# Attention and mixture of experts on one core: from all experts over all rows to experts over rows sorted by routing

## The reference

```python
def reference(x, ...):                       # x: (32, 256, 128) float32
    # attention: 16 heads of size 8
    qkv = (x @ W_qkv.T + b_qkv).reshape(B, T, 16, 24)
    att = softmax(einsum('bthd,bshd->bhts', q, k) / sqrt(8))
    x = layernorm(x + einsum('bhts,bshd->bthd', att, v) @ W_out.T + b_out)
    # mixture of 8 experts, 2 for each row, and one shared expert
    scores = sigmoid(x @ gate_w.T)
    sel = top_k(scores + expert_bias, 2)
    top_scores = scores at sel
    for each row and each of its 2 experts e:
        routed = row * score
        h = silu(routed @ w1[e].T) * (routed @ w3[e].T)
        out_r = (h @ w2[e].T) * score
    shared = silu(x @ sw1.T) * (x @ sw3.T) @ sw2.T
    return layernorm(x + shared + sum of the row's two out_r)
```

## Time and profile before

| | |
|---|---|
| profiled execution | 847.3 us, of it 845.5 us span |
| median of the runs | 844.6 us |
| PE | 762.4 us (90%), 6228 matmuls |
| VectorE | 708.3 us (84%) |
| ScalarE | 579.6 us (69%) |
| POOL | 472.3 us (56%) |
| DMA | 109.36 MB, mean 129 GB/s |
| last gate logits | 469 us |

### The profile page before, as it was taken

The page is one execution under the profiler, slowest core; times in us unless marked ns, Lnnn a source line. Parts: engine busy times, 40 slices in busy tenths (PEclk is TensorE's granted clock), DMA queues, the critical chain, the costliest instruction groups (busy, mean ns, idle before and its releaser), DMA issues.

```text
span 845.5 us, 19602 instructions
## 1 busy us (share of the span) xinstructions
PE 762.4 (90%) x6228; PEld 472.6 (56%) x6228; DVE 708.3 (84%) x1430; ACT 579.6 (69%) x1192; POOL 472.3 (56%) x687
## 2 busy tenths in 40 slices
PE   2598999999999999999987889989999999999894
PEld 1234555555555555555545566666666666666662
DVE  5577999999999999999983688888888787887885
ACT  1038999998989999899884566555555655565551
POOL 3336654554555456455212466666766766666664
PEclk9998999999999999999998899999999999999997
DMA  5754767676777677676412633334444544444430
GB/s 156 161 121 105 168 170 168 148 167 169 164 155 178 149 165 167 171 161 144 103 34 68 172 91 91 107 99 104 119 119 110 124 124 124 124 124 121 116 86 26
DMA packets 201682, 109.36 MB, mean 129 GB/s; under 512 B 10496, under 2 KB 201088, under 8 KB 201600
## 3 DMA queue, kind: packets, MB, share of 16 engines
q1 hardware_dynamic: 200048, 105.88, 51.7%
q10 hardware_dynamic: 1552, 2.44, 1.0%
HBM read 73.94 MB, written 33.82 MB: 127 GB/s over the span
## 4 chain that ended last, share of the span: by engine, by line
PE 60%; DVE 11%; POOL 9%; issue 8%; DMA 7%; ACT 2%; SPq 1%; DVEq 1%; POOLq 0%; ACTq 0%
PE bank L732 15%; PE bank L704 10%; PE bank L717 7%; DMA probs<-route_dram 5%; PE bank L739 4%; PE bank L741 3%; PE bank L740 3%; DVE k_stack L1083 3%; POOL place L510 3%; POOL rstd L519 3%; PE bank L814 2%; PE bank L897 2%; PE bank L794 2%; PE bank L834 2%; PE bank L801 2%
## 5 line engine op out<-in xcount | busy, mean ns | idle before, releaser
L1009 DVE TENSOR_REDUCE negmax<-bank 128x2 f32<-128x512 f32 x512 | 320.3, 679 | 31.2 <-PE bank L717 28.7
L558 ACT ACTIVATE probs<-bank 128x512 f32<-128x512 f32 x512 | 291.4, 606 | 44.8 <-PE bank L704 41.1
L717 PE MATMUL bank<-k_stack,q_stack 48*128 48x256 bf16 x1024 | 164.2, 284 | 11.4 <-DMA k_stack<-k_parts_dram 7.3
L704 PE MATMUL bank<-q_stack,k_stack 50*128 50x256 bf16 x1024 | 158.0, 276 | 7.6 <-ACT probs L558 6.1
L739 PE MATMUL bank<-x_hi,hi_w 128*128 128x512 f32 x288 | 137.6, 478 | 14.8 <-DVE k_stack L1083 9.5
L732 PE MATMUL bank<-probs,v_aug 128*32 128x256 f32 x2048 | 139.4, 390 | 0.4 <-ACT attT L569 0.4
L1073 DVE TENSOR_TENSOR k_stack<-bank,probs 128x512 f32<-128x512 f32 x128 | 87.6, 684 | 49.1 <-DMA probs<-route_dram 31.5
L704 PEld LDWEIGHTS bank<-q_stack,k_stack 50*128 50x128 bf16 x1024 | 75.6, 95 | 92.5 <-ACT probs L558 48.5
L741 PE MATMUL bank<-x_lo,hi_w 128*128 128x512 f32 x288 | 114.4, 397 | 0.0
L740 PE MATMUL bank<-x_hi,lo_w 128*128 128x512 f32 x288 | 114.0, 396 | 0.0
L510 POOL TENSOR_TENSOR k_stack<-k_stack,probs 128x512 f32<-128x512 f32 x48 | 62.0, 1293 | 79.1 <-DVE k_stack L1083 71.3
(11 more groups left out here) (116 smaller groups left out, 1338.7 us busy)
## 6 DMA issues: line engine op xcount, KB each, us to landing
probs<-route_dram SPq DMA_DIRECT2D x128, 256.0 KB, 6.0
q_stack<-q_parts_dram SPq DMA_DIRECT2D x64, 192.0 KB, 3.7
k_stack<-k_parts_dram SPq DMA_DIRECT2D x64, 192.0 KB, 4.9
k_parts_dram<-k_parts SPq DMA_DIRECT2D x32, 192.0 KB, 2.2
q_parts_dram<-q_parts SPq DMA_DIRECT2D x32, 192.0 KB, 2.2
xT_sb<-xT SPq DMA_DIRECT2D x32, 128.0 KB, 2.2
k_parts_dram<-k_parts SPq DMA_DIRECT2D x32, 128.0 KB, 2.0
q_parts_dram<-q_parts SPq DMA_DIRECT2D x32, 128.0 KB, 2.2
```

Source lines behind the costliest of these rows:

```text
L558: nc.scalar.activation(probs[h][:], score_ps[EXP_BANK[h]][:].rearrange("p (j t) -> p j t", j=NT), ACT.Exp).then_inc(exp_done, 1)
L704: mm = pe.matmul(score_ps[EXP_BANK[h]][:, j * T:(j + 1) * T], k_stack[b.ring][first:last, h // 2, j * P:(j + 1) * P], q_stack[b.ring][firs ...
L717: mm = pe.matmul(max_ps[MAX_BANK[h]][:, i * T:(i + 1) * T], q_stack[b.ring][first:last, h // 2, i * P:(i + 1) * P], k_stack[b.ring][first: ...
L1009: nc.vector.tensor_reduce(negmax[b.ring % 2][:, :, column], max_ps[MAX_BANK[h]][:].rearrange("p (i s) -> p i s", i=NT), AX_X, ALU.max, neg ...
```

## The change

Each expert now sees only its rows. The 32 batches are cut into five chunks of 6, 8, 8, 6 and 4 batches (12, 16, 16, 12 and 8 tiles). When the logits of a chunk are there, VectorE routes it in 26 small steps spread over the heads of one slot, four slots after the chunk's last batch (slots 9, 17, 25 and 31; the last chunk's after the slots): both choices as before, then running counts of each expert's rows, and for each row the two places in a DRAM table (rows_dram) in which every expert's rows stand in blocks of 128. Two small bf16 matmuls add the counts over partitions. Empty places must be blank: ScalarE's queue writes zeros to the tables, two quads a slot from slot -2. POOL sends each tile's rows (132 numbers wide: 128, and the score) with indirect DMAs, one per tile and choice, 128 in all: four a slot (two before x_bo, two at the end), eight from slot 28 on. The copy into x1T, x1_dram and the products of slot 33 go.

```diff
+        def scatter_plan():
+
+            queue, plan = [], {}
+            for s in range(-4, B + 3):
+                for c in chunks[:-1]:
+                    if s == c.last + ROUTE_SLOT + 1:
+                        queue += [(c, choice, i) for choice in range(2) for i in range(c.n)]
+                for place in range(2):
+                    many = 2 if s < B - 4 else 4
+                    plan[s, place], queue = queue[:many], queue[many:]
+            return plan, queue + [(chunks[-1], choice, i) for choice in range(2) for i in range(chunks[-1].n)]
+
+        SCATTERS, LAST_SCATTERS = scatter_plan()
```

```diff
+            def scatter(c, choice, i):
+                if i == 0 and choice == 0:
+                    pool.wait_ge(route_step, steps(c, 23))
+                    pool.wait_ge(blanked[c.c], 16 * c.quads)
+                if i == 0 and choice == 1:
+                    pool.wait_ge(rows_out[c.c][0], 16 * c.n)
+                if i == 0:
+                    pool.tensor_copy(x1_rows[:, c.t0:c.t0 + c.n, C], scores_of(c, choice)).then_inc(score_put, 1)
+                    pool.wait_ge(score_put, 2 * c.c + choice + 1)
+                pool.indirect_dma_start(c.rows_dram, bass.IndirectOffsetOnAxis(ap=slot_column(c, choice, i), axis=0),
+                                        x1_rows[:, c.t0 + i, :], None).then_inc(rows_out[c.c][choice], 16)
+
+            def scatters(s, place):
+                if s == 1 and place == 0:
+                    tables()
+                for c, choice, i in SCATTERS[s, place]:
+                    scatter(c, choice, i)
...
+                scatters(t.s, 0)
...
-                if b.live:
-                    pool.wait_ge(x1T_set, b.count(1, 1))
-                    pool.tensor_copy(x1T[:, bass.ds(b.n * T, T)], x1T_new[:]).then_inc(x1T_kept, 1)
+                            pool.tensor_tensor(w_lo[m][:], w_stage[m][:], w_hi[m][:], ALU.subtract).then_inc(w_lo_set, 1)
+                scatters(t.s, 1)
 
             slots(pool, slot)
...
+            for c, choice, i in LAST_SCATTERS:
+                scatter(c, choice, i)
+
+            def gather(g):
+
+                c = chunk_of_group(g)
+                if g == c.groups[0]:
+                    for r in range(2):
+                        pool.wait_ge(y_kept[r], kept(c, r))
+                if g >= GY:
+                    pool.wait_ge(combined, 2 * GT * (g - GY + 1))
+                for choice in range(2):
+                    for i in range(GT):
+                        column = slot_column(c, choice, g * GT + i - c.t0)
+                        pool.indirect_dma_start(gathered[g % GY][:, choice * GT + i, :], None, c.y_dram,
+                                                bass.IndirectOffsetOnAxis(ap=column, axis=0)).then_inc(gather_in[g % GY], 16)
+
+            def root(c):
+                pool.wait_ge(eps2_set, c.c + 1)
+                tiles = slice(c.t0, c.t0 + c.n)
```

```diff
+            def load_rows(k):
+                c = chunk_of_quad(k)
+                for choice in range(2):
+                    sp.wait_ge(rows_out[c.c][choice], 16 * c.n)
+                if k == 0:
+                    for other in chunks:
+                        sp.wait_ge(blanked[other.c], 16 * other.quads)
+                if k >= XQ:
+                    sp.wait_ge(xT_T, k - XQ + 1)
+                    sp.wait_ge(hid_set, 4 * (k - XQ + 1))
+                q = k - c.k0
+                sp.dma_start(xq[k % XQ][:], c.rows_dram[4 * P * q:4 * P * (q + 1), :].rearrange("(a p) c -> p a c", p=P)
+                             ).then_inc(xq_in[k % XQ], 16)
+
+            def keep_products(k):
+                c = chunk_of_quad(k)
+                q = k - c.k0
+                sp.wait_ge(yq_set, k + 1)
+                sp.dma_start(c.y_dram[4 * P * q:4 * P * (q + 1), :].rearrange("(a p) c -> p a c", p=P),
+                             y_q[k % 2].rearrange("p (a c) -> p a c", c=C)).then_inc(y_kept[k % 2], 16)
```

```diff
+            def blanks(first):
+                for k in range(max(first, 0), min(first + BLANKS, QUADS)):
+                    c = chunk_of_quad(k)
+                    if k == 0:
+                        act_e.wait_ge(blank_set, 1)
+                    act_e.dma_start(c.rows_dram[4 * P * (k - c.k0):4 * P * (k - c.k0 + 1), :].rearrange("(p a) c -> p a c", a=4),
+                                    xq[0][:]).then_inc(blanked[c.c], 16)
...
+            def rows_to_sbuf(k):
+                act_e.wait_ge(xT_T, k + 1)
+                if k >= 2:
+                    act_e.wait_ge(up_mm, 4 * (k - 1))
+                nc.scalar.activation(xT_q[k % 2], xT_ps[:], ACT.Copy).then_inc(xT_set, 1)
+
+            def silu_of(k):
+                if k >= 2:
+                    act_e.wait_ge(hid_set, 4 * (k - 1))
+                act_e.wait_ge(xq_in[k % XQ], 16 * (k // XQ + 1))
+                for a in range(4):
+                    act_e.wait_ge(up_mm, 4 * k + 2 * (a // 2) + 2)
+                    nc.scalar.activation(silu[k % 2][:, a * P:(a + 1) * P], up_ps[a // 2][:, a % 2 * 2 * C:a % 2 * 2 * C + C], ACT.Silu,
+                                         scale=xq[k % XQ][:, a, C:C + 1]).then_inc(silu_set, 1)
+
```

```diff
-                if past(g, 1) or n >= DEPTH:
-                    pe.wait_ge(hid_set, done(g, n - DEPTH))
-                if n == 0:
-                    pe.wait_ge(x_lo_set, g + 1)
-                product(up1_ps[n % DEPTH], 0, n, x_hi[r], x_lo[r]).then_inc(up_mm, 1)
-                product(up3_ps[n % DEPTH], 1, n, x_hi[r], x_lo[r]).then_inc(up_mm, 1)
...
-            def down(g, n, r):
...
-                    pe.matmul(down_ps[r][:], w2_whole[:, n, :], (hid_s if n else hid)[n % DEPTH], start=(n == 0), stop=(n == NE - 1)).then_inc(down_mm, 1)
-                    return
-                wait_lo(pe, g, n)
-                n %= NE
-                product(down_ps[r], 2, n, hs_hi[n % DEPTH], hs_lo[n % DEPTH], start=(n == 0), stop=(n == NE - 1)).then_inc(down_mm, 1)
...
+            def experts(k):
+                c = chunk_of_quad(k)
+                pe.wait_ge(route_step, steps(c, ROUTE_STEPS))
...
+            def up(k):
+                pe.wait_ge(xT_set, k + 1)
+                if k:
+                    pe.wait_ge(hid_set, 4 * k)
+                else:
+                    pe.wait_ge(exp_done, H * B)
+                    pe.wait_ge(max_red, H * B)
+                for a in range(4):
+                    pe.matmul(up_ps[a // 2][:, a % 2 * 2 * C:a % 2 * 2 * C + 2 * C], xT_q[k % 2][:, a * P:(a + 1) * P],
+                              wall_up[:, bass.ds(first_column(k, a), 2 * C)], start=True, stop=True).then_inc(up_mm, 1)
+
+            def hidden_turned(k):
+                pe.wait_ge(hid_set, 4 * k + 4)
+                if k:
+                    pe.wait_ge(hidT_set, k)
+                for a in range(4):
+                    mm = pe.transpose(hidT_ps[:, a * P:(a + 1) * P], hid[k % 2][:, a * P:(a + 1) * P], ident[:])
+                mm.then_inc(hid_T, 1)
+
+            def down(k):
+                pe.wait_ge(hidT_set, k + 1)
+                if k:
+                    pe.wait_ge(yq_set, k)
+                for a in range(4):
+                    mm = pe.matmul(y_ps[:, a * P:(a + 1) * P], hidT[k % 2][:, a * P:(a + 1) * P],
+                                   wall_down[:, bass.ds(first_column(k, a), C)], start=True, stop=True)
+                mm.then_inc(down_mm, 1)
+
...
+            def step(k):
+                if k + 1 < QUADS:
+                    rows_turned(k + 1)
+                if 0 < k <= QUADS:
+                    hidden_turned(k - 1)
+                if k < QUADS:
+                    experts(k)
+                    up(k)
+                if 0 < k <= QUADS:
+                    down(k - 1)
+                if k == 0:
+                    pe.wait_ge(exp_done, H * B)
+                    counts_over_rows(chunks[-1], sT_ps)
+                for g in shared_in(k, 2):
+                    shared_down(g)
+                for g in shared_in(k, 1):
+                    shared_up(g)
+                for g in shared_in(k, 0):
+                    shared_turned(g)
+
```

```diff
-            def weigh(g, n):
-
-                e = n - 1
-                dve.wait_ge(up_mm, g * (2 * NE) + (2 * n + 1))
-                if past(g, 1) or n > DEPTH:
-                    dve.wait_ge(act_set, done(g, n - DEPTH))
-                dve.wait_ge(weight_in[e], g * 16 + 16)
-                nc.vector.tensor_tensor(gated[n % DEPTH], up1_ps[n % DEPTH][:], weight_b[e], ALU.mult).then_inc(gated_set, 1)
...
+            def hidden_to_sbuf(k):
+                dve.wait_ge(hid_T, k + 1)
+                if k >= 2:
+                    dve.wait_ge(down_mm, k - 1)
+                nc.vector.tensor_copy(hidT[k % 2], hidT_ps[:]).then_inc(hidT_set, 1)
+
+            def hidden(k):
+                if k >= 2:
+                    dve.wait_ge(hid_T, k - 1)
+                for a in range(4):
+                    dve.wait_ge(silu_set, 4 * k + 2 * (a // 2) + 2)
```

(32 more changed lines are left out.)

790 lines of the change are left out of this document (395 added, 395 removed).

## The result

The changed kernel took 908.46 us (four runs, 901.98 to 912.91) against 845.76 us of the kernel before (840.38 to 847.2): ratio 1.0748, 95% interval 1.0666 to 1.083. It was slower by 7%, where 777 us had been forecast. The same program then ran on other chips: on chips 5 and 6 it took 761 to 766 us, on chip 14 again 913 (the chip of the recorded runs is not known). On chip 11 only variants of it ran; the four took 753 to 763 us. The kernel before takes 842 to 848 us in the median on all of them. So there are two results to explain. The document shows first the profile of the recorded one, then the one of chip 6.

The account below looks back on a forecast made before the run. VectorE was taken to bound attention, PE's three-part products the experts. Last logits at 498, quads ending at 738 and a tail gave 778, or 777 us on the median of runs, with 715 to 845 as the 8-in-10 range.

Parts of the forecast that it names:

- POOL's DMA pieces about 1.3 us apart: Sign for the forecast: each scatter or gather costs POOL 1.3 us, which fits its idle places in attention.
- Rival A: POOL's price: at 2.0 us a scatter or gather, POOL sets the pace and the end is 878; chance 0.09.
- Rival B: DMA crowding: blank writes and scatters delay 20 attention slots by 24 us, quad loads add 23; together 825; chance 0.16.
- last logits: End of attention: the last gate logits come at 498 us, +- 8, where the kernel before had 469.
- Routing: VectorE's added work in attention: 7.6 us for 12 tiles, 9.6 for 16, 27 in sum; chunk 3 nothing.
- Scatters: POOL's row sends in attention: 6 us of lateness over 20 slots, and 4 more in slots 32 to 34.
- what left the stretch: Work gone from attention: twelve early up matmuls, 4 us, and weight splits now 128 wide, 4 us.
- Steps: The 42 expert quads: 4.7 us each in steps 0 to 11, 5.5 to 5.8 after; ending at 738 us.
- rival C: Small operations cheap, register load hidden by transposes: expert steps of 4.1, 4.8 and 5.0, time 745; chance 0.20.
- The register load: Reading four expert numbers into PE registers each quad: 0.9 us with the address steps, from nothing to 2.2.
- a sign of being wrong in kind: No POOL idle in slots of 120 to 400 us, chunk 3 gathers outlasting the quads, or PE waiting for xq loads.
- Tail: After the last quad: copy and landing 3, last 16 gathers 21, landing 2.5, combine to out write 13; end 778.

Follow-up runs that it names:

- all-plain run: Changed kernel with all 256 indirect DMAs of POOL made plain DMAs of the same bytes, rows in order: 739.0 us (chip 6), 737.8 (chip 5), 735.7 (chip 10).
- e5_few: Changed kernel issuing only 10 of 128 scatters and 16 of 128 gathers: 729.2 us on chip 6, 727.7 on chip 10.
- e1_const: Changed kernel with constant weight addresses in the quads' matmuls; the compiler dropped the register load too: 760.0 us on chip 11, 900.6 on chip 10.
- the reordered one: Changed kernel with POOL's scatters and gathers in another order, none in slots 32 to 34, everything computed: 757.1 us on chip 5, ratio 0.8962.

## Why the prediction was wrong, and where it was right

**The step that failed** is the one that took POOL's DMAs for a cost of POOL alone: "POOL's DMA pieces about 1.3 us apart", with queueing behind them and their bytes as the only harm to others. On chips 10 and 14, and where the recorded result was taken, a run of indirect DMAs also makes PE's semaphore updates late, and what waits for them waits up to 19 us at a time. Where it is seen the same program takes 913 us (chip 14), where not, 761 (chip 6). No rival had this. Rival A came nearest in time (878), by a price of 2.0 us; the price was 1.26, and POOL was not the bound: from 520 us on in the recorded profile it waited 112 us for written products. Rival B (DMA crowding) is excluded as the cause by the all-plain run. On chips 5 and 6 the time, 761 to 766 us, lies inside the stated range, 11 to 16 us under the forecast, and there the sum can be checked term by term.

**What of it holds on undisturbed chips** (chip 6, span 757.6, forecast 778):

- Attention: last logits at 497.2, forecast 498. Routing cost 8.0 us for 12 tiles and 8.9 and 7.9 for 16 (two slots each, of 19.7 and 12.9, 20.5 and 13.0, 19.6 and 12.9 against 12.3), forecast 7.6 and 9.6, summing to 25 against 27. Scatters cost some 15 (run e5_few), of which the forecast had 6 + 4; what left the stretch was then worth some 12 (469 + 25 + 15 less 497), forecast 8. The sum was right by two errors of opposite sign.
- Steps: 1 to 11 took 4.54 us, 12 to 41 5.08, forecast 4.7 and 5.5 to 5.8. From the last logits to the copy of the last quad's products (707.9) it is 211 us, forecast 240: this is the term that was mis-sized, by 29 us; rival C had 4.1 and 4.8 to 5.0. The register load is the largest part. With its address steps it was put at 0.9 us a step, 38 us in all. Between the first up products of quads 0 and 41 the three undisturbed runs without the load (in e1_const without the address steps too) take 199.7 to 200.3 us, the changed kernel 202.7 to 204.6 on chips 5 and 6: it costs 3 to 5 us in all, 0.1 a step. The load itself takes 0.33 us in the recorded profile (least, median, most in ns):

```profile
L932 PEldq TENSOR_LOAD <-expert_of x42: 327/332/649, 522.7 to 837.9; - x42
```

The Trainium skill, "DMA: Bandwidth & Descriptors" (Latency and other measured facts), has a floor of about 600 ns for it; the measurement of four registers is below that and decides. Its 1 us for the emission by GpSimd agrees with the 0.96 us that POOL is held, but not with the distance of 1.26.

What made good for part of it in steps 1 to 11: PE stands 6.2 us for a quad's rows between 505 and 555 us, which the prediction had at nothing and, if "there" means the quads, named as a sign of being wrong in kind. From step 12 on VectorE does not set the pace, as the forecast of 5.8 had it. Its eight additions take 2.3 us, not 3.0, and it is busy for 113 of 143 us, where PE is begun for 137:

```profile
560.00:703.00 143.00, 137.19 (x902) 121.84 (x901) 113.31 (x363) 91.66 (x222) 88.90 (x88) 1.00 0.58 156
```

- Tail: 50 us after that copy, forecast 40. POOL gathers from 643 to 744 us with only pows between, 72 gathers of 1.26 and 8 us of pow: the gathers of chunk 3 were not over when the last quad was written. The prediction had named that as a sign of being wrong in kind; the tail is 10 us longer.

- POOL's indirect DMAs took 0.94 to 0.96 us in the median in every run that has at least 128 of them, 1.24 at most, with VectorE 45% or 79% busy beside them. The Trainium skill, "SBUF — State Buffer" (the "DVE blocks DMA" trap), says that GpSimd cannot write a DMA's descriptors while VectorE is in an operation of a two-port mode; no run here shows the trap.

**What stays open.** That the indirect form is needed is shown side by side on chip 10, up to the order of the rows. How an indirect DMA makes PE's semaphore updates late is not shown. Nor is it shown that the chip makes the difference: each chip was used at its own time (the runs on chips 11, 6 and 5 before those on 14 and 10), so what else went on there can be the cause as well. Eight scatters in a row from 506 us and eight gathers from 866 us in the recorded profile had no late wait beside them; PE made few updates then (two are recorded from 506 to 518 us), which fits, but shows nothing. The changed kernel itself was not run on chips 10 and 11, nor the reordered one where the disturbance is seen.

## What to carry to other kernels

An indirect DMA on POOL can cost the engines around it more than its 1.26 us: where a closed chain PE to ScalarE to VectorE runs, keep long runs of them out of it, or plan them as time in which the chain stands. Before a difference between two variants is believed, run the unedited kernel beside them on the same chip: here four edits on chip 11 seemed to cure a stall, and two of them had it again on chips 10 and 14. And a kernel that wins 10% on two chips and loses 7 to 8% elsewhere has no single time; judge it over chips. Where a profile puts waits down to an unknown event, look at what happens long before the suspected part: late waits stood in attention too, where no register is loaded.
